# A gated cross-attention and expert-choice layer on one core: the first batch's expert choice at six places per quad of tiles, with its slots and gathers beside the last quad

## The reference

```python
x = x + tanh(g_xattn[0]) * xattn(layernorm(x), ctx, mask)      # q, k, v, softmax over 77, output projection
xn = layernorm(x)
probs = softmax(xn @ gate_w.T, axis=-1)                        # 8 experts
g, m = top_k(probs.transpose(0, 2, 1), 512)                    # per batch and expert: 512 of 2048 tokens
xin = xn[batch, m]
h = gelu(xin @ w1[e], approximate=False) @ w2[e]               # 512 -> 2048 -> 512
x = x + tanh(g_ffn[0]) * scatter_add(m, g * h)
```

## Time and profile before

| | |
|---|---|
| median of 3 runs | 1584.35 us (1581.07 to 1585.58) |
| the profiled execution | 1584.71 us |
| its span, first to last instruction | 1583.0 us |
| mean granted clock of TensorE | 0.981 |
| busy: PE, DVE, ACT, POOL | 1504.1, 1015.0, 749.4, 573.8 us |

### The profile page before, as it was taken

The page is one execution under the profiler, slowest core; times in us unless marked ns, Lnnn a source line. Parts: engine busy times, 40 slices in busy tenths (PEclk is TensorE's granted clock), DMA queues, the critical chain, the costliest instruction groups (busy, mean ns, idle before and its releaser), DMA issues.

```text
span 1583.0 us, 22317 instructions
## 1 busy us (share of the span) xinstructions
PE 1504.1 (95%) x7153; PEld 1215.4 (77%) x7153; DVE 1015.0 (64%) x1704; ACT 749.4 (47%) x1399; POOL 573.8 (36%) x541
## 2 busy tenths in 40 slices
PE   6887588999999999999999999999999999999996
PEld 6444367788788888888888888888888888888885
DVE  1378777556866766576766667576667665766542
ACT  1775133345544545454444454455445454554432
POOL 1265622453444234432444135404442344323311
PEclk9998699999999999999999999999999999999998
DMA  6075522462333442334323434243334423442133
GB/s 230 23 271 195 165 72 80 114 173 80 80 107 92 89 111 83 107 81 108 95 92 81 95 93 121 61 108 86 107 94 87 115 80 107 81 107 80 40 79 68
DMA packets 101479, 163.71 MB, mean 103 GB/s; under 512 B 7418, under 2 KB 45318, under 8 KB 101365
## 3 DMA queue, kind: packets, MB, share of 16 engines
q1 hardware_dynamic: 86965, 128.66, 26.1%
q0 software_dynamic: 14400, 33.56, 11.5%
HBM read 128.64 MB, written 33.55 MB: 102 GB/s over the span
## 4 chain that ended last, share of the span: by engine, by line
PE 85%; DVE 7%; ACT 3%; issue 2%; POOL 1%; DMA 1%; POOLq 0%; SPq 0%; ACTq 0%; DVEq 0%
PE bank L1289 41%; PE bank L1175 33%; PE bank L1149 3%; PE bank L1444 1%; PE bank L544 1%; PE bank L562 1%; DVE w2hl L1134 1%; PE bank L392 1%; DVE count L816 1%; DVE st L781 1%; DVE onehot L1330 1%; DVE atleast L863 1%; DMA ctx_raw<-in_ctx 0%; PE bank L414 0%; ACT xT L612 0%
## 5 line engine op out<-in xcount | busy, mean ns | idle before, releaser
L1289 PE MATMUL bank<-w2hl,hh 128*128 128x512 f32 x2048 | 637.6, 393 | 0.0
L1175 PE MATMUL bank<-xo,whl 128*128 128x512 f32 x2352 | 544.4, 390 | 3.8 <-DVE mix L1239 2.8
L1175 PEld LDWEIGHTS bank<-xo,whl 128*128 128x128 f32 x2352 | 442.1, 188 | 98.5 <-DVE mix L1239 3.7
L1289 PEld LDWEIGHTS bank<-w2hl,hh 128*128 128x128 f32 x2048 | 381.6, 188 | 76.2
L1289 PE MATMUL bank<-w2hl,hid_low 128*128 128x512 f32 x1024 | 399.6, 390 | 0.0
L1289 PEld LDWEIGHTS bank<-w2hl,hid_low 128*128 128x128 f32 x1024 | 192.9, 188 | 40.5
L1394 POOL DMA_INDIRECT layer_out<-y,slot_row x64 | 102.5, 1601 | 302.0 <-ACT y L1309 287.2
L1134 DVE TENSOR_TENSOR w2hl<-raw,w2hl 128x512 fp32r<-128x512 f32 x226 | 160.7, 732 | 54.3 <-ACT w2hl L1129 45.8
L1103 POOL TENSOR_TENSOR whl<-raw,whl 128x512 fp32r<-128x512 f32 x56 | 82.2, 1468 | 260.2 <-ACT whl L1069 260.2
L1129 ACT ACTIVATE w2hl<-raw 128x512 fp32r<-128x512 f32 x228 | 136.5, 624 | 59.9 <-DMA raw<-in_L_ffn_w 41.0
L1108 POOL TENSOR_TENSOR whl<-wsum,whl 128x512 fp32r<-128x512 f32 x56 | 75.0, 1340 | 183.4 <-ACT whl L1090 183.4
(11 more groups left out here) (221 smaller groups left out, 1808.3 us busy)
## 6 DMA issues: line engine op xcount, KB each, us to landing
raw<-in_L_ffn_w SPq DMA_DIRECT2D x228, 256.0 KB, 2.7
raw<-in_L_ffn_w SPq DMA_DIRECT2D x72, 512.0 KB, 4.9
x_s<-in_x SPq DMA_DIRECT2D x8, 1024.0 KB, 6.9
layer_out<-x SPq DMA_DIRECT2D x8, 1024.0 KB, 9.0
xn_rows<-xn SPq DMA_DIRECT2D x8, 1024.0 KB, 4.7
raw_k<-in_L_xattn_Wk SPq DMA_DIRECT2D x1, 1024.0 KB, 5.3
raw_q<-in_L_xattn_Wq SPq DMA_DIRECT2D x1, 1024.0 KB, 11.6
raw_v<-in_L_xattn_Wv SPq DMA_DIRECT2D x1, 1024.0 KB, 13.6
```

The source lines that it names most:

```text
L1175: last = pe.matmul(bk[:, :], whl[:, p % 2, part, 2 * w + k, :], xo[:, xpart, x, k, :], start=(not adds and k == 0 and part == HIGH and xpa ...
L1289: last = pe.matmul(Y_BANKS[c][:, :], high if hpart == HIGH else low[:, c * P:(c + 1) * P], w2hl[:, f % 4, part, :], start=(s == 0 and hpar ...
```

## The change

Six places per quad instead of three, in every iteration: on PE after the second and the fourth turn of x, inside the scores, and after the weighings 1, 2 and 3; on DVE at the start, after two weighings, after the maximum, after the other two weighings, within the statistics and after them. `between` does one piece at each, and its list now has 14 entries: the 12 pieces, then the tables of expert 0 with the slots' product on PE, then the slots. PE turns token blocks 0 and 1 in iteration 8 ahead of the exponentials of quad 7, and blocks 2 and 3 after its second weighing. DVE splits blocks 0 and 1 ahead of the first two weighings of quad 7 and blocks 2 and 3 behind them. ACT copies all four after the first high part of the weights in iteration 8, and then goes on to the rest. POOL gathers ahead of the low part of the weights. `spare` becomes a tile of its own, in memory that `xp` takes later, for which ACT waits until the squares are done.

```diff
+        spare = overlay("spare", [P, Q, D], BF16)
         xp = overlay("xp", [P, B, 2, KD, CAP], F32R)
...
-            spare = onehot[:, :, :].rearrange("p (q t) s -> p q (t s)", q=Q)
...
-        CHOOSE_FROM, PLACES = QB + 1, 3
+        CHOOSE_FROM, PLACES = QB + 1, 6
...
     # attention_pe
                         last.then_inc(turned, 1)
-                between(it - 1, 1)
+                        if i == 1:
+                            between(it - 1, 3)
+                    between(it - 1, 4)
+                if it == NQ:
+                    pe.wait_ge(sc_ready, NQ)
+                    for c in (0, 1):
+                        tokens_pe(pe, 0, c)
                 q = it - 1
                 if q >= 0:
                     pe.wait_ge(exped, q + 1)
...
                         if k == 2:
-                            between(it - 1, 2)
+                            between(it - 1, 5)
                     last.then_inc(turned, 1)
-                else:
-                    between(it - 1, 2)
...
-                    if i == 1:
-                        between(it, 0)
-            between(NQ, 1)
+                    if i >= 1:
+                        between(it, i - 1)
+                    if i == 1 and it == NQ:
+                        for c in (2, 3):
+                            tokens_pe(pe, 0, c)
...
     # attention_act
                 if it == NQ:
                     w1_high_act(act, 0, 0, 0)
+                    for c in range(NC):
+                        first_tokens_act(act, c)
...
     # attention_pool
                 if it == NQ:
-                    w1_low_pool(pool, 0, 0, 0)
                     for c in range(NC):
                         gather_pool(pool, 0, 0, c)
+                    w1_low_pool(pool, 0, 0, 0)
                     promote_pool(pool, 0, 0)
...
     # attention_dve
                 between(it, 0)
                 if 0 <= it - 1 < NQ:
+                    if it == NQ:
+                        for c in (0, 1):
+                            split_tokens_dve(dve, 0, c)
                     for i in (0, 1):
                         weigh(it - 1, i)
+                    if it == NQ:
+                        for c in (2, 3):
+                            split_tokens_dve(dve, 0, c)
+                between(it, 1)
...
                        .then_inc(smax_ready, 1)
+                between(it, 2)
                 q = it - 1
                 if 0 <= q < NQ:
                     for i in range(2, Q):
                         weigh(q, i)
-                between(it, 1)
-                if it == NQ:
-
-                    hot_dve(dve, 0, 0)
-                    slots_dve(dve, 0, 0)
+                between(it, 3)
...
                         own.mark(dve.bn_stats(st2[:, i, :], x1[:, q % 2, i, :]))
+                        if i == 1:
+                            between(it, 4)
...
-                between(it, 2)
-
-            for c in (0, 1):
-                split_tokens_dve(dve, 0, c)
+                between(it, 5)
+
             logits_out(NQ - 1)
...
     # beside_attention
             def between(it, place):
                 at = (it - CHOOSE_FROM) * PLACES + place
-                if it == NQ and place > 0:
-                    pieces = range(at, N_PIECES) if place == 1 else ()
+                if 0 <= at < N_PIECES + 2:
+                    do(at)
+            return between
+
+        def first_choice_dve(dve, own):
+            def do(piece):
+                if piece < N_PIECES:
+                    choice_dve(dve, own, 0, piece)
+                elif piece == N_PIECES:
+                    hot_dve(dve, 0, 0)
                 else:
-                    pieces = range(at, at + 1) if 0 <= at < N_PIECES else ()
-                for piece in pieces:
-                    do(0, piece)
-            return between
+                    slots_dve(dve, 0, 0)
+            return do
+
+        def first_choice_pe(pe):
+            def do(piece):
+                if piece < N_PIECES:
+                    choice_pe(pe, 0, piece)
+                elif piece == N_PIECES:
+                    slots_pe(pe, 0)
+            return do
...
         def first_tokens_act(act, c):
+            if c == 0:
+                act.wait_ge(squares_done, NQ)
             act.wait_ge(x_turned, c + 1)
...
     # after attention_act
-            for c in range(NC):
-                first_tokens_act(act, c)
...
     # after attention_dve
             choice_start_dve(dve, own, 1)
-            for c in (2, 3):
-                split_tokens_dve(dve, 0, c)
             choice_dve(dve, own, 1, 0)
...
     # after attention_pe
-            slots_pe(pe, 0)
-            for c in range(NC):
-                tokens_pe(pe, 0, c)
             hidden_pe(pe, 0, 0)
```

More of the change, by code:

```diff
@@ L1860, in _ @@
                                            ALU.logical_shift_right))
-            attention_dve(dve, own, beside_attention(lambda b, n: choice_dve(dve, own, b, n)))
+            attention_dve(dve, own, beside_attention(first_choice_dve(dve, own)))
             choice_start_dve(dve, own, 1)
-            for c in (2, 3):
-                split_tokens_dve(dve, 0, c)
             choice_dve(dve, own, 1, 0)
@@ L1875, in _ @@
             prep_pe(pe)
-            attention_pe(pe, beside_attention(lambda b, n: choice_pe(pe, b, n)))
-            slots_pe(pe, 0)
-            for c in range(NC):
-                tokens_pe(pe, 0, c)
+            attention_pe(pe, beside_attention(first_choice_pe(pe)))
             hidden_pe(pe, 0, 0)
```

## The result

The changed kernel takes 1592.29 us (median of 5 runs, 1590.25 to 1594.6), the kernel before 1584.35 us (5 runs, 1581.07 to 1585.58). The measured ratio is 1.0064, 95% interval 1.0048 to 1.0080; the two medians alone are 7.94 us apart, 0.50%, at the low end of that interval. One later run each of the kernel before and of the variant e6 took about 2180 us at a granted clock of 0.65, and the ratios leave both out. The profiled execution took 1592.29 us, with a span of 1590.6 against 1583.0.

The account below looks back on a forecast made before the run. DVE's serial work up to the first piece of batch 1's choice was taken to set the end: +6.8 us there and +1.2 us of clock on 1584.7 us gave 1592.7, stated as 1592.5 us, range 1583 to 1599.

Parts of the forecast that it names:

- DVE up to quad 6's statistics: DVE in attention: 12.35 us more work ahead, 2.3 us of idle time saved; statistics ready at 168.0 us (165.8 to 170.3).
- POOL's 6.93 us: POOL's time from quad 6's statistics to the end of its normalization, which the gathers follow: 6.93 us, done at 175.0.
- The gather's 3.59 us: From the first gather's issue on POOL to PE's use: 3.59 us, taken from the trace before.
- Behind the turn: From tokens 0 and 1 turned (181.7): exponentials, copies, splits and weighings, to quad 7's statistics at 193.3 and logits at 196.3.
- the marker: End of the first piece of batch 1's choice on DVE: moves from 197.0 to 203.8 us, +6.8 us (4 to 9).
- The first piece: First piece of batch 1's choice on DVE: 6.77 us as before, beside a busy POOL; starts at 197.0, ends at 203.8.
- The clock at the first output block: TensorE's first output block may run at the lower clock after PE stands still: 0 to 2.6 us, taken as 1.2.
- I carry its shift to the end at full size: Loop of PE, ACT and DVE waits on nothing outside itself, so the shift of the first piece's end reaches the kernel's end.
- the 8.0: Forecast sum for the whole kernel: +6.8 us of shift and +1.2 us of clock, +8.0 us.
- Costed at nothing: Scratch tile's place, PE's first hidden block start, POOL's low parts, SP's later weight load, PE's extra count waits: no cost.
- the faster one: Rival: packing the choice wins if the first gather is issued before about 166 us; -7.1 us, 1577.3 us; chance 0.12.

Follow-up runs that it names:

- e6: Changed kernel with SP holding back quad 6's normalized rows and the second weight tile's load behind them until the four gathers landed; ratio 1.0059.
- e1b: Changed kernel with POOL's four gathers one iteration earlier, ahead of quad 6's normalization, and PE's first token wait adapted; 1581.77 us, ratio 1.0003.
- e2: Changed kernel with the first tokens' turns, copies and splits put back behind quad 7, as in the kernel before; 1580.88 us, ratio 0.9992.
- e3: Changed kernel with SP's load of the second weight tile moved to right behind the first tile's load; 1590.99 us, ratio 1.0063.
- e7: Changed kernel with 18 unused matmuls on PE in the stall ahead of the first token turn; 1588.37 us, ratio 1.0049.
- e5: Changed kernel with POOL's gathers ahead of quad 6's normalization and the first tokens' work behind quad 7; 1577.88 us, ratio 0.9982.
- e8: Kernel before with only the sums' scratch tile in its own memory and POOL's gathers ahead of the first weight tile's low part; 1579.83 us, ratio 0.9993.
- e10: Changed kernel with gathers ahead of quad 6's normalization and token blocks 0 and 1 turned behind quad 7's exponentials; 1574.64 us, ratio 0.9969.
- e9: As e10, with SP also holding back the first two w2 blocks and quad 6's sums until the gathers landed; 1580.12 us, ratio 0.9995.

## Why the prediction was right, and which of its steps were not

Forecast 1592.5 us, measured 1592.29. That the two are 0.2 us apart is luck: the interval of the ratio is 5 us wide, and several terms of the sum were wrong by 1 to 4 us in both directions. The mechanism stood: POOL's order holds the gathers, PE waits ahead of quad 7's exponentials, DVE behind it, and batch 1's choice is late. e1b and e2 show it by taking it away in two ways. Step by step:

- **DVE up to quad 6's statistics**: forecast 168.0, measured 168.64. The choice had begun 0.91 us earlier, so the way there was 1.5 us longer than forecast: 0.8 us of idle time was saved instead of 2.3, if the work is as I counted it. (DVE's idle time over those 40.5 us was 5.0, not 4.5.)
- **POOL's 6.93 us**: it took 170.79 + 3.02 - 168.73 = 5.08. In the kernel before, two of its rows ran beside a comparison of DVE (L863), and another normalization, quad 7's, beside other work of DVE:

```profile
158.66 1.09 DVE L863 TENSOR_TENSOR atleast<-prob,cand 128x896 bf16<-128x896 f32 x1
...
161.90 1.09 DVE L863 TENSOR_TENSOR atleast<-prob,cand 128x896 bf16<-128x896 f32 x1
```

POOL in the same trace:

```profile
158.69 1.96 POOL L661 TENSOR_TENSOR norm<-norm,powers 128x4 f32<-128x4 f32 x1
...
187.39 3.08 POOL L705 TENSOR_SCALAR xn<-x,norm 128x512 f32<-128x512 f32 x4
```

Beside the comparison the power takes 1.96 us and the four normalizations 3.94; in the changed kernel, with no comparison there, they take 1.04 and 3.02, and quad 7's took 3.08 beside DVE's other rows. So the 1.85 us are two comparisons at 0.92 each, and the change had moved them away from there. Together with the shorter step to the gather (0.17 instead of 0.6) the first gather was 1.6 us earlier than forecast, 173.98.
- **The gather's 3.59 us: this step failed.** It took 7.61. I had counted each transfer of SP for its own cover and not as a neighbour of the gathers, although quad 6's rows are released by the same engine's last row that releases the gathers. e6 gives the size: 4 us, of which e3 shows 1 for the load. Against the 1.6 us of the line above, 2.4 remain at PE's first use (181.59, forecast 179.2), and 1.8 at the end of the turns of tokens 0 and 1 (183.5, forecast 181.7), since the second block was there already. (What the prediction says of the Trainium skill here, DMA: Bandwidth & Descriptors, Anatomy of one DMA, takes the fixed cost of about 2.0 us alone. The section adds a term for the bytes; with 256 KB its formula gives an estimate of 2.6 us, so the sum would have come out 1.0 us lower, not 1.6. The gathers took 3.5 to 3.7 us with nothing beside them.)
- **Behind the turn**: two splits at 186.47 (forecast 185.0), statistics of quad 7 at 196.5 (193.3). Of these 3.2 us, 1.5 were there at the splits; the rest is the weighing at PE's lower clock, a term that I had put only behind the marker. e7 sizes it, token turns and all, at 2.9.
- **The first piece**: forecast 6.77 beside a busy POOL, took 203.97 + 1.75 - 199.96 = 5.76. The marker, read at PE's count right behind it, moved by 205.79 - 197.04 = 8.75, forecast 6.8 (4 to 9). From the start of the choice it is 9.7, outside those bounds.
- **The clock at the first output block**: I took 1.2 of 0 to 2.6. The granted clock is 0.51 from 204 to 211 us, and from the count to the third hidden block PE needed 212.37 - 205.84 = 6.5 us where it had needed 201.27 - 197.08 = 4.2. Of these 2.3 us, 1.0 is taken back by a shorter wait for the second count (1.34 instead of 2.39). The net, 11.48 - 10.18 from the first count to the second, is 1.3, where I took 1.2, but it is made up otherwise: the output block itself cost 1.1 (3.83 us against 2.72), the six hidden matmuls ahead of it, which I had not priced, 1.3 (2.91 against 1.63), and the shorter wait gave 1.0 back. The same 11.5 us stand in all eight traces in which PE waits 4.2 to 6.3 us for the first count, and the 10.2 in the four in which it waits 0.4 at most (before, e2, e5, e8).
- **"I carry its shift to the end at full size": this step failed too.** 8.75 + 1.3 = 10.05 us at the second count became 8.5 at the separation and 8.3 at the start of expert 1 (399.15 against 390.84), and 7.6 at the end of the profiled pair. The loop waits for nothing outside itself, but its rounds are not of fixed length: the changed trace has one slow round fewer, 1.6 us. With the trace of e8 as the yardstick the separation moved by 13.4 us, not 9.4; the timed ratio, 1.0064, is 10.1 us, between the two. So the 8.0 met the 7.94 between the first medians partly because the trace that I started from had two slow rounds.
- **Costed at nothing**: right for the scratch tile and POOL's low part, as far as e8 can tell (to about 2 us, and in the old order). POOL's low part ended at 188.5, forecast 187.

Of the rivals, the faster one had the right deciding point but too large a price: with the gathers issued at 162.28, before the 166 us named, the forecast of 1577.3 became 1581.8, ratio 1.0003 (e1b), since the gathers land late there as well. With PE's order mended too (e10) it is 0.31% below the kernel before, 4.9 us; the 7.1 us of that rival lie just inside the interval (to 7.9 us).

What stays open: whether the loop's slow rounds are more frequent behind a long wait of PE. All six traces with the tokens ahead of the exponentials have one or two, e2, e5, e8, e9 and e10 none, but the kernel before has two; one trace each does not settle it. The times of e3 and e6, which differ from the changed kernel's by less than their intervals, leave open how much of a 3 us earlier count reaches the end.

## What to carry to other kernels

When work is pulled forward on one engine, follow its product to the next queue: the slots were 16 us earlier, but the gathers stood in POOL's order behind work whose input came later than before, and what counts is the last wait ahead of the issue. Do not put a wait for a transfer ahead of independent work on an in-order engine; put it where the engine waits anyway (e10). And price a transfer by what is issued in the same microsecond beside it, not by its duration on a quiet queue.

## What the runs showed of the hardware that was not expected

- An indirect gather of 128 rows of 2 KB landed in 3.5 to 3.7 us alone, and in 5.5 to 7.5 us when a 1 MB store had been issued 0.15 us ahead of it and a 512 KB load 0.27 us behind. With both held back (e6) PE had the first after 3.61 us, and the fourth landed in 3.7; with the load alone away (e3) it was 6.45 and 4.3.
- PE's lower clock after 17.6 us of idle time cost 2.9 us: the granted clock was 0.52 over the 9 us behind the wait (181.6 to 190.7 us) and 1.00 after that. It is shown by filling the wait with 15.7 us of unused matmuls.
- POOL's 128x512 normalization of four tiles took 3.02 us beside an idle DVE and 3.08 beside several of DVE's other operations, but 3.94 when one 128x896 comparison of DVE fell into it; a 128x4 power took 1.96 us instead of 1.04 the same way. In the changed kernel two normalizations took 3.71 us (at 156.66) beside the one-hot table of 2.28 us. Which property of these two operations does it is not tested.
